# One 128 by 128 product of k with itself per head and tile in place of three groups of small block products

## What is computed

```python
q = _l2norm(q)
k = _l2norm(k)
v = v * beta[..., None]
kb = k * beta[..., None]
q, k, v, kb = map(rs, (q, k, v, kb))              # chunks of 32
A = -jnp.tril(jnp.einsum('bhncd,bhned->bhnce', kb, k), -1)
eye = jnp.eye(chunk, dtype=q.dtype)
T = solve_triangular(eye - A, jnp.broadcast_to(eye, A.shape), lower=True)
u = T @ v
w = T @ kb
```

## Time and profile before

| what | value |
|---|---|
| median of 3 runs | 1384.86 us (1383.08 to 1401.52) |
| the profiled execution's own time | 1372.92 us |
| its span, first to last instruction | 1371.2 us |
| mean granted TensorE clock | 0.920 of full |
| TensorE matmuls busy | 1152.8 us, 84% |
| VectorE busy | 811.1 us, 59% |
| ScalarE busy | 532.3 us, 39% |
| GpSimd busy | 393.6 us, 29% |

### The profile page before, as it was taken

How to read it: one execution, slowest core, us unless ns; L and a number is a source line. 1 busy time by engine, 2 the same in 40 slices (tenths; PEclk the granted TensorE clock), 3 DMA queues, 4 the chain that set the end, 5 groups by cost and what they waited for, 6 DMA issues and landing times.

```text
span 1371.2 us, 27484 instructions
## 1 busy us (share of the span) xinstructions
PE 1152.8 (84%) x10204; PEld 835.5 (61%) x10204; DVE 811.1 (59%) x1542; ACT 532.3 (39%) x849; POOL 393.6 (29%) x597
## 2 busy tenths in 40 slices
PE   3686897889978997889977998888978999888837
PEld 3543773578537874478635884477734895467526
DVE  5752464765757464765747566665647657663353
ACT  1143244523534335523545334523454225522322
POOL 6008103900066101921057100931029100750000
PEclk9998898999989998999989999999989999986658
DMA  4040104010311004010121004010040203010000
GB/s 137 16 93 3 28 16 93 11 37 1 84 25 30 19 16 92 2 30 18 51 59 29 19 17 92 1 30 18 16 93 1 46 1 78 17 30 16 1 1 16
DMA packets 80265, 47.47 MB, mean 35 GB/s; under 512 B 55808, under 2 KB 73728, under 8 KB 80128
## 3 DMA queue, kind: packets, MB, share of 16 engines
q1 hardware_dynamic: 80128, 45.56, 14.4%
HBM read 30.86 MB, written 14.68 MB: 33 GB/s over the span
## 4 chain that ended last, share of the span: by engine, by line
PE 55%; DVE 22%; ACT 9%; issue 8%; SPq 3%; POOL 2%; DMA 1%; DVEq 0%; ACTq 0%; POOLq 0%
PE psum L747 11%; PE psum L748 9%; PE psum L749 9%; DVE conv_acc L1315 5%; PE psum L778 5%; DVE arena L1547 3%; PE psum L932 2%; DVE h_hi L1294 2%; PE psum L917 2%; PE psum L951 2%; PE psum L956 2%; SPq L342 2%; PE psum L1116 2%; DVE arena L1549 2%; PE psum L873 1%
## 5 line engine op out<-in xcount | busy, mean ns | idle before, releaser
L511 POOL TENSOR_TENSOR l_prod<-arena 64x30 f32<-64x30 f32 (+14 forms) x240 | 146.4, 610 | 628.9 <-DMA arena<-l_dram 610.7
L564 ACT ACTIVATE h_f<-psum,b_col 128x512 f32<-128x512 f32 x128 | 87.9, 687 | 287.4 <-PE psum L749 254.7
L747 PE MATMUL psum<-w_hi,h_hi 128*128 128x256 f32 x512 | 153.4, 300 | 24.9 <-DVE h_lo L1295 24.9
L515 POOL TENSOR_TENSOR arena<-arena,l_prod 64x30 f32<-64x30 f32 (+14 forms) x240 | 144.6, 602 | 18.8
L749 PE MATMUL psum<-w_hi,h_lo 128*128 128x256 f32 x512 | 145.6, 284 | 0.0
L748 PE MATMUL psum<-w_lo,h_hi 128*128 128x256 f32 x512 | 145.5, 284 | 0.0
L1294 DVE CAST h_hi<-h_f 128x512 fp32r<-128x512 f32 x128 | 81.4, 636 | 102.4 <-ACT h_f L564 53.8
L1315 DVE SCALAR_TENSOR_TENSOR conv_acc<-psum,conv_col,conv_acc 128x511 f32<-128x511 f32 x144 | 107.8, 748 | 56.7 <-ACT conv_acc L589 47.7
L747 PE MATMUL psum<-xt_hi,w_hi 128*128 128x512 f32 x256 | 113.6, 444 | 31.1 <-DVE xt_lo L1281 13.0
L1052 PE MATMUL psum<-v_shift,fir_w 128*32 128x512 f32 x1152 | 125.3, 593 | 0.0
L747 PEld LDWEIGHTS psum<-w_hi,h_hi 128*128 128x128 f32 x512 | 98.3, 192 | 32.8 <-issue 16.2
(11 more groups left out here) (228 smaller groups left out, 2274.5 us busy)
## 6 DMA issues: line engine op xcount, KB each, us to landing
x_in<-in_L_attn_x SPq DMA_DIRECT2D x8, 512.0 KB, 5.0
v_dram<-v_fm SPq DMA_DIRECT2D x8, 512.0 KB, 2.8
v_shift<-v_dram SPq DMA_DIRECT2D x8, 512.0 KB, 5.0
out<-x_tok SPq DMA_DIRECT2D x8, 512.0 KB, 3.8
v_shift<-v_dram SPq DMA_DIRECT2D x8, 511.0 KB, 7.0
v_shift<-v_dram SPq DMA_DIRECT2D x8, 510.0 KB, 9.2
v_shift<-v_dram SPq DMA_DIRECT2D x8, 509.0 KB, 11.7
arena<-in_L_ffn_w SPq DMA_DIRECT2D x2, 1024.0 KB, 7.2
```

Of the source, the lines that this page charges most:

```text
L511: pool.tensor_tensor(prod, l_inv[:, k + 1:, k:k + 1].broadcast_to(shape), l_inv[:, k:k + 1, 0:k].broadcast_to(shape), ALU.mult).then_inc(i ...
L515: pool.tensor_tensor(l_inv[:, k + 1:, 0:k], l_inv[:, k + 1:, 0:k], prod, ALU.add).then_inc(inverted, 1)
L564: act.activation(h_f[:, m % 2, :], bank, ACT.Gelu, bias=b1_col[:, m:m + 1]).then_inc(read, 1)
L747: pe.matmul(dst, a_hi, b_hi, start=first, stop=False, **kw)
```

## The change

The three groups of small products of k with itself (gram: 32 by 32 diagonal blocks; lhalf: 64 by 64; lpair: 64 by 32) go. In k_rows TensorE now makes one 128 by 128 product per head and tile, 16 in all, with the helper that also makes the attention products (tile_products). They fill four banks, 0, 1, 3 and 4. VectorE reads all parts from them at once: eight products of 32 partitions for l_tok, the mask, then under_diagonal: for r = 1 and then r = 0 two products of 32 partitions into l_pair and one of 64 partitions into l_half. Only behind each r are its two banks freed. For room, "rows" moves from bank 3 to 7, "rows_t" from 3 to 2, and q0 and q1 trade banks (7 and 4). l_half and l_pair move to other SBUF space, so they can be written before the FIR is done.

```diff
--- before.py
+++ after.py
@@ -112,9 +112,7 @@
-        l_half = v_shift[D:P, 2:4, 32:WIDE].rearrange("p g (u j) -> p g u j", j=D)
-        l_pair = v_shift[:, 4, 32:WIDE].rearrange("p (u j) -> p u j", j=CHUNK)
@@ -124,7 +122,9 @@
-        l_turned = sb("l_turned", [CPT * UNITS, CHUNK, CHUNK])
+        under = sb("under", [P, CHUNK * CHUNK])
+        l_turned = under[0:CPT * UNITS, :].rearrange("p (i j) -> p i j", i=CHUNK)
+        l_half = under[D:P, :].rearrange("p (g u j) -> p g u j", g=2, j=D)
@@ -137,6 +137,7 @@
+        l_pair = hm[:, 1, :].rearrange("p (u j) -> p u j", j=CHUNK)
@@ -174,20 +175,20 @@
-        K = [("k", (0, 1)), ("rows", (3,)), ("gram", (0, 1)), ("rows_t", (3,)), ("q", (4, 7)), ("k_t", (2, 5)), ("hidden", (3,))]
+        GRAM = (0, 1, 3, 4)
+        K = [("k", (0, 1)), ("rows", (7,)), ("gram", GRAM), ("rows_t", (2,)), ("q", (7, 4)), ("k_t", (2, 5)), ("hidden", (3,))]
...
-        Q = [("lhalf", (0, 1)), ("rows_q", (2,)), ("rows_qt", (5,)), ("at", (4, 7) * 2)]
+        Q = [("rows_q", (2,)), ("rows_qt", (5,)), ("at", (4, 7) * 2)]
...
-        L_OFF = [("lpair", (0, 1))]
@@ -973,18 +979,8 @@
-                grams = [claim(pe, at, "gram", b) for b in range(2)]
-                pe.sem_inc(passed, 1)
-                for u in range(UNITS // 2):
-                    t, half = u // HALVES, u % HALVES
-                    for c in range(CPT):
-                        cols = slice(P * t + CHUNK * c, P * t + CHUNK * c + CHUNK)
-                        for b in range(2):
-                            rows = slice(D * b, D * b + D)
-                            last = pe.matmul(grams[b][0][32 * c:32 * c + 32, 32 * u:32 * u + 32], qk_fm[rows, half, 0, cols],
-                                             qk_fm[rows, half, 0, cols], start=True, stop=True)
-                            if u == UNITS // 2 - 1 and c == CPT - 1:
-                                last.then_inc(grams[b][1], 1)
+                for r in range(2):
+                    tile_products(at, "gram", r, 0)
@@ -1008,36 +1004,19 @@
-            def attend(at, r):
-                banks = [claim(pe, at, "at", 2 * r + p) for p in range(2)]
+            def tile_products(at, what, r, second):
+
+                banks = [claim(pe, at, what, 2 * r + p) for p in range(2)]
                 pe.sem_inc(passed, 1)
                 for n in range(4):
                     t, half = 2 * r + n // 2, n % 2
                     toks = slice(P * t, P * t + P)
                     for p in range(2):
                         rows = slice(D * p, D * p + D)
-                        last = pe.matmul(banks[p][0][:, P * n:P * n + P], qk_fm[rows, half, 0, toks], qk_fm[rows, half, 1, toks],
-                                         start=True, stop=True)
+                        last = pe.matmul(banks[p][0][:, P * n:P * n + P], qk_fm[rows, half, 0, toks],
+                                         qk_fm[rows, half, second, toks], start=True, stop=True)
...
-            def off_diagonal(at, what):
...
@@ -1151,22 +1130,19 @@
-                    off_diagonal(at, "lhalf")
                     q_rows_turn(at)
                     pe.wait_ge(silu_made, 6 * j + 6)
-                    attend(at, 0)
+                    tile_products(at, "at", 0, 1)
...
-                if at.front:
-                    off_diagonal(at, "lpair")
...
@@ -1477,14 +1451,42 @@
-                    for b in range(2):
-                        bank, read = arrive(dve, at, "gram", b)
-                        shape = [P, UNITS // 2, CHUNK]
-                        link(dve.tensor_tensor(l_tok[:, b::2, :], bank[:, 0:UNITS // 2 * CHUNK].rearrange("p (u j) -> p u j", j=CHUNK),
-                                               c2n[:, b::2].unsqueeze(2).broadcast_to(shape), ALU.mult))
-                        dve.sem_inc(read, 1)
+
+                    for r in range(2):
+                        for p in range(2):
+                            arrive(dve, at, "gram", 2 * r + p)
+                        dve.sem_inc(passed, 1)
+                        for c in range(CPT):
+                            rows = slice(CHUNK * c, CHUNK * c + CHUNK)
+                            last = dve.tensor_tensor(by_parity(l_tok, rows, r), products(r, rows, CHUNK * c, CHUNK),
+                                                     unit_scale(rows, r, CHUNK), ALU.mult)
+                    link(last)
...
+                def under_diagonal():
+                    for r in (1, 0):
+                        for q in range(2):
+                            rows = slice(D * q + CHUNK, D * q + D)
+                            dve.tensor_tensor(by_parity(l_pair, rows, r), products(r, rows, D * q, CHUNK),
+                                              unit_scale(rows, r, CHUNK), ALU.mult)
+                        rows = slice(D, P)
+                        link(dve.tensor_tensor(l_half[:, r, :, :].rearrange("x (n p) j -> x n p j", p=2), products(r, rows, 0, D),
+                                               unit_scale(rows, r, D), ALU.mult))
+                        for p in range(2):
+                            _, read = where_read(at, "gram", 2 * r + p)
+                            dve.sem_inc(read, 1)
...
-                def off_diagonal(what):
...
@@ -1524,6 +1513,7 @@
                     k_rows()
+                    under_diagonal()
                     conv(4)
@@ -1587,16 +1577,12 @@
-                    off_diagonal("lhalf")
...
-                    off_diagonal("lpair")
...
```

More of the change, by code:

```diff
@@ L245, in arrive, with where_read @@
             eng.wait_ge(filled[b], fills)
+            return BANKS[b], emptied[b]
+        def where_read(at, what, k=0):
+            b, _, _ = content(at, what, k)
             return BANKS[b], emptied[b]
@@ L316, in macaron_kernel @@
         T_LOADS = CPT + 2 * (CPT - 1)
-        DVE_STEPS = {"head": 48, "body": 81, "last": 76, "tail": 38}
+        DVE_STEPS = {"head": 49, "body": 82, "last": 77, "tail": 38}
         CONST_MADE, C_LOADED, SETUP_DVE = 57, 57, 30
@@ L1018, in attend @@
                         rows = slice(D * p, D * p + D)
-                        last = pe.matmul(banks[p][0][:, P * n:P * n + P], qk_fm[rows, half, 0, toks], qk_fm[rows, half, 1, toks],
-                                         start=True, stop=True)
+                        last = pe.matmul(banks[p][0][:, P * n:P * n + P], qk_fm[rows, half, 0, toks],
+                                         qk_fm[rows, half, second, toks], start=True, stop=True)
                         if n == 3:
                             last.then_inc(banks[p][1], 1)
-            def off_diagonal(at, what):
-                banks = [claim(pe, at, what, p) for p in range(2)]
-                pe.sem_inc(passed, 1)
-                wide = what == "lhalf"
-                for u in range(UNITS // 2):
-                    t, half = u // HALVES, u % HALVES
-                    for q in (1,) if wide else (0, 1):
-                        later = slice(P * t + D * q, P * t + D * q + D)
-                        sooner = slice(P * t, P * t + D) if wide else slice(P * t + D * q, P * t + D * q + 32)
-                        width = D if wide else CHUNK
-                        for p in range(2):
-                            rows = slice(D * p, D * p + D)
-                            last = pe.matmul(banks[p][0][D * q:D * q + D, width * u:width * u + width],
-                                             qk_fm[rows, half, 0, later], qk_fm[rows, half, 0, sooner], start=True, stop=True)
-                            if u == UNITS // 2 - 1 and q == 1:
-                                last.then_inc(banks[p][1], 1)
             def firs(at, a):
@@ L1486, in k_rows, with products, by_parity @@
+                    link(last)
                     dve.tensor_tensor(l_tok[:, :, :], l_tok[:, :, :],
                                       low_strict[:, :].unsqueeze(1).broadcast_to([P, UNITS, CHUNK]), ALU.mult).then_inc(l_made, 1)
+                def products(r, rows, col, width):
+                    return psum[rows, GRAM[2 * r]:GRAM[2 * r] + 2, :].rearrange("x p (n m) -> x n p m", m=P)[:, :, :, col:col + width]
+                def by_parity(dst, rows, r):
+                    return dst[rows, 8 * r:8 * r + 8, :].rearrange("x (n p) j -> x n p j", p=2)
@@ new lines, in unit_scale @@
+                def unit_scale(rows, r, width):
+                    return c2n[rows, 8 * r:8 * r + 8].rearrange("x (n p) -> x n p", p=2).unsqueeze(3) \
+                        .broadcast_to([rows.stop - rows.start, 4, 2, width])
+                def under_diagonal():
[10 more added lines that the diff above has]
+                            dve.sem_inc(read, 1)
@@ L1498, in q_inverse @@
                     dve.reciprocal(inv[:, 1, :], nrm[:, 1, :])
-                def off_diagonal(what):
-                    for p in range(2):
-                        bank, read = arrive(dve, at, what, p)
-                        if what == "lhalf":
```

(7 more changed lines are left out.)

14 lines of the change are left out of this document (5 added, 9 removed).

## The result

| | before | changed |
|---|---|---|
| median of 4 runs, us | 1386.2 (1383.1 to 1401.5) | 1439.2 (1430.6 to 1456.2) |
| profiled execution, us | 1372.9 | 1430.6 |
| its span, us, and mean granted clock | 1371.2, 0.920 | 1428.9, 0.884 |

The ratio is 1.034, with a 95% interval of 1.022 to 1.046: slower. The median lies 13 us above the forecast of 1426 and inside the range. One of the four changed runs (1456.2 us) counts as slow and is left out of the ratio; the median of the other three is 1431.9 us.

A forecast was written before the change was run, and what follows sets the result against it. TensorE's stream, matmuls busy 84% of the span, was taken to set the pace. Body passes +27.5, last pass +11.2 and head +2.3 made about +41 us, moving the 1384.9 us median to 1426, range 1398 to 1445.

The forecast's parts named there:

- Rows moved to bank 7: L968 waits for VectorE's hidden(0): TensorE idles 3.6 us, half clock for 2.8 us costs 1.4, L993 starts 4.7 us late.
- The stall gone: The unexplained 4.74 us gap inside the q0 projection, most likely an instruction fetch, disappears; not a term of its own.
- VectorE ahead of q1: Between L993 and q1: eight l_tok products 3.4 us, then mask and under_diagonal; 6.0 us from first product to bank 4's release.
- Old L993 to the logits: From the old start of the rows' transpose L993 to the gate's logits L1116: 18.6 us, against 13.4 in pass 3.
- The last pass: The final pass, 6.3 us from L993 to the logits before: +12.3 us, less 1.1 saved later, 11.2 in all.
- The head pass: Bank 7 is free there; l_made comes 2.3 us later and shows in full at the merge: +2.3 us.
- The body passes: Six passes: 3 x 5.2 + 5.7 + 2 x 6.4 = 34.1 us later logits, less 6 x 1.1: +27.5 us.
- -1.1 in each of seven passes: In FFN C, where TensorE has no gap, dropping lpair's 64 records saves 1.1 us net per pass.
- it will be a later cast that waits as long: GpSimd's later last writes of the inverse still meet FFN C's casts; the first took 4.71 us, a later one would; price 0.
- B: Rival, still slower: half clock lasts longer, or the fetch stalls elsewhere, 4.7 us in six passes; 1454 to 1468 us; chance 0.17.
- A: Rival, within 2%: TensorE keeps full clock through its new waits, VectorE's products follow at 0.34 us; about 1401 us; chance 0.22.
- C: Rival, faster: the stall's 28 us are won because VectorE's 14 new instructions cost almost nothing; 1350 us; chance 0.04.

The follow-up runs named there:

- the fourth experiment: The changed kernel with idle products that nobody reads filling TensorE's two new waits in the body and last passes: 1408.4 us, ratio 1.021 to the kernel before.
- the sixth experiment: The changed kernel with the eight l_tok products ordered by partition, r = 0 and r = 1 of the same partitions behind one another: one run, 1418.1 us.

## Why the prediction was right

It named the two waits, their releasers and their effect on the logits, and the experiments show that these are the cause. That the sum came near is in part luck, as the terms show.

- *Rows moved to bank 7.* A gap of 3.6 us was forecast and 3.37 came, with half clock for 3.5 us (2.8 taken). Two errors met here. The twelve records of L974 and L978 were put at 5.46 us at full clock and took 3.58 us in the fourth experiment: when the bank comes free the squares are long ready, and four records of L978 run beside the last four of L974 (552.63 and 552.64 above). The half clock cost 1.7 to 2.7 us on top of that, not 1.4. The rows' transpose was 3.1 to 4.2 us late instead of 4.7.
- *The stall gone.* So it was.
- *VectorE ahead of q1.* From the first product to q1's start 6.0 us were forecast and came. Eight products were put at 3.4 us and took 3.46. The products that start at other partitions did not overlap, as the Trainium skill has it ("VectorE: DVE Perf Modes", section "Two Vector instructions with no wait between them"), and the sixth experiment shows the other side, 3.07.
- *Old L993 to the logits.* 18.6 us were forecast. L993 stood 10.6 us behind the store, so 27.9 to 29.0 make 17.3 to 18.4. The last pass lost 11.25 where 12.3 stood.

The sum was 41 us on the profiled execution and 57.7 came. By stretches, cut at the eight stores of v (the first belongs to the head pass, the last to the last pass):

| stretch | forecast | measured |
|---|---|---|
| up to the head pass's store | 0 | +5.4 |
| from there to the first body pass's | +2.3 | +4.3 |
| six times from store to store | +27.5 | +41.5 |
| from the last pass's store to the end | +11.2 | +6.5 |

**The setup** has no changed instruction. It lost 5.4 us because TensorE was at half clock for longer; changed and before, 50 us into the span:

```profile
50.00:83.00 33.00, 27.61 (x118) 23.14 (x118) 21.80 (x45) 7.35 (x10) 0.00 (x0) 0.66 0.06 16
```

```profile
50.00:78.00 28.00, 19.30 (x115) 15.82 (x114) 21.56 (x46) 7.57 (x11) 0.00 (x0) 0.94 0.06 19
```

That is chance between executions and should have widened the range, not moved the forecast: in ten of the eleven experiments' traces the first store stands at 77.3 to 78.9 us, in one at 83.3, as here at 83.7. **The head pass**: l_made came 4.1 us later behind its store, not 2.3. Its L978 ran at half clock in this execution, 3.49 us against the 1.90 of the same four records in the earlier trace rows, which makes 1.6 of the difference and had no term in the prediction:

```profile
89.63 3.49 PE L978 MATMUL psum<-arena,kq_sel 128*32 128x512 f32 x4 [3.85 <-ACT arena L684]
```

From the head's merge to the next store both kernels took 59.4 us, but in eight of the experiments this stretch, which no edit touches, took 64.7 to 67.6: one execution of each can't settle a few us here.

**The body passes** are the term that was mis-sized. Up to the logits they lost 3.9 to 6.1 us each, 30.8 together where 34.1 was forecast. But "-1.1 in each of seven passes" for lpair did not arrive. From the query rows to the merge one body pass gained 1.1 us and the others lost 1.2 to 2.5, together 8.6; behind the merge 2.0 more were lost. In pass 3 half clock around the start of FFN C lasted 6.8 us instead of 3.4:

```profile
608.30:615.10 6.80, 4.93 (x15) 3.95 (x16) 1.97 (x5) 2.69 (x4) 5.69 (x14) 0.50 0.01 2
```

(the changed kernel, pass 3). In pass 3 the merge had half clock for about 10 us more, and that pass took 169.6 us against 157. The small gaps of 0.84 and 0.92 us stand just ahead, but the filler for one of them didn't bring the time back; why the clock was lower there stays open. The traces show how much of it can be chance. From the query rows to the merge, six passes together, the time is 265.0 us before and 273.6 in the changed kernel, and 258.0 to 281.3 in the experiments; the two with the old kernel and its loads of v moved have 263.9 and 273.6. So neither lpair's gain of 6.6 us nor this loss of 8.6 can be told from one execution of each. **The last pass** gained 4.7 us between the query rows and the merge, where 1.1 was forecast and "it will be a later cast that waits as long" was expected. GpSimd was already in its last write when the first long cast came: the cast took 2.63 us where 5.61 stood, and the gap ahead of FFN C's products shrank from the first row (before) to the second (changed). That sentence was wrong there.

```profile
1222.63 0.39 PE L747 MATMUL psum<-w_hi,h_hi 128*128 128x256 f32 x1 [2.67 <-DVE h_lo L1295]
```

```profile
1279.14 0.39 PE L753 MATMUL psum<-w_hi,h_hi 128*128 128x256 f32 x1 [0.26 <-DVE h_lo L1269]
```

Among the rivals, B (the stall at another place) did not occur, and full clock through the new waits, as in A, occurred only where it was forced. C was refused for the right reason: the stall can be won only if q1 doesn't wait for VectorE, and 1363 to 1343 us is what that gives; 1350 had been worked out. The Trainium skill ("Runtime: NRT & Kernel Launch", section "Instruction fetch mechanics") calls a crossing mostly hidden. If the stall is one, this case differs: 4.24 to 4.76 us in each of six passes.

## What to carry to other kernels

When a change needs more banks at one time, list for each bank number who reads it last before, and where that reader stands in its own engine's order: here the same instructions took 1432 or 1363 us by the bank numbers alone. An idle gap on TensorE ended by nothing, next to a burst of loads that fills all DMA engines, is worth a trial with the loads issued later; one wait on SP gained 46 us, more than the whole rewrite at its best. Price the gaps that a change opens on TensorE with the half clock that went with like gaps in the trace (here 3.37, 4.74 and 6.29 us), and expect differences from the clock at places that the change doesn't touch: here they came to 5 us in the setup.

## What was not expected of the hardware

- With loads under way that nobody waited for yet, TensorE stood still for 4.24 to 4.76 us in each of six passes; issuing them later took 46 to 51 us off 1385. With the new products in place of the small ones the same loads stopped nothing.
- Feeding TensorE products that nobody reads, 38 in a pass, took 24 us off.
- Products of two kinds that write different 32 partitions of one bank ran in pairs when both were ready: twelve records took 3.58 us instead of 5.46.
- VectorE's 32-partition products of 256 elements start 0.43 us apart when they change partitions and 0.1 us less when they don't.
